# Last stage of a vision-transformer kernel: the layer norm's affine step and residual fused on VectorE over PSUM

## The reference, cut to what matters

```
z    = (h2 - mean(h2)) * rsqrt(var(h2) + eps)
r    = z + w_first * expert_out[first] + w_second * expert_out[second]
out  = h2 + (r - mean(r)) * rsqrt(var(r) + eps) * gamma + beta
```

## Time and profile before

| | us |
|---|---|
| median of 3 runs | 2032.84 |
| lowest, highest run | 2028.87, 2034.92 |
| span of the profiled execution | 2037.3 |
| first product of the last stage's matmuls used by DVE | 1877.96 |
| last DVE instruction of the stage ends | 2028.63 |

### The profile page before, as it was taken

The page is one execution under the profiler, slowest core; times in us unless marked ns, Lnnn a source line. Parts: engine busy times, 40 slices in busy tenths (PEclk is TensorE's granted clock), DMA queues, the critical chain, the costliest instruction groups (busy, mean ns, idle before and its releaser), DMA issues. The chain is left out here.

```text
span 2037.3 us, 49150 instructions
## 1 busy us (share of the span) xinstructions
PE 1498.2 (74%) x12152; PEld 991.7 (49%) x12153; DVE 1431.0 (70%) x3551; ACT 1376.4 (68%) x3956; POOL 1162.3 (57%) x1903
## 2 busy tenths in 40 slices
PE   6999957856656565663688885888865999994663
PEld 6999954411111111111344443555534988884553
DVE  2544559978777777776466666888876777774896
ACT  1323224429999999997799994777753766663885
POOL 2333330046666666662455552677775888884997
PEclk9999978955555555555555555555556999997786
DMA  7654310002222222221544445444433555554785
GB/s 293 258 231 193 160 39 1 1 32 83 85 75 76 76 87 75 84 78 49 136 138 150 143 146 152 132 154 154 154 123 107 140 140 137 146 144 143 224 271 159
DMA packets 184974, 263.32 MB, mean 129 GB/s; under 512 B 28372, under 2 KB 147363, under 8 KB 180328
## 3 DMA queue, kind: packets, MB, share of 16 engines
q1 hardware_dynamic: 137456, 202.16, 31.8%
q0 software_dynamic: 19840, 39.17, 5.4%
q10 hardware_dynamic: 27540, 20.52, 3.1%
HBM read 149.17 MB, written 108.01 MB: 126 GB/s over the span
## 5 line engine op out<-in xcount | busy, mean ns | idle before, releaser
L956 ACT ACTIVATE exps_summed<-s,neg_shift 128x197 f32<-128x197 f32 x1184 | 481.9, 535 | 32.4 <-POOL neg_shift L830 30.4
L956 ACT ACTIVATION_READ_ACCUMULATOR exps_summed<-s,neg_shift (+1 forms) x1184 | 339.0, 317 | 0.0
L993 DVE TENSOR_REDUCE score_max<-s 128x788 f32 (+3 forms) x320 | 285.9, 893 | 66.5 <-PE s L900 58.7
L1353 ACT ACTIVATE exps<-st,scalars 128x788 f32<-128x788 f32 (+1 forms) x320 | 246.4, 891 | 17.6 <-PE st L1262 17.5
L2034 POOL DMA_INDIRECT expert_sums<-y_tile,row_places x216 | 218.4, 1011 | 60.9 <-issue 28.9
L384 PE MATMUL mm<-w_tok,x_transposed 128*128 128x192 f32 x1176 | 209.4, 328 | 0.8 <-ACT x_transposed L345 0.8
L345 ACT COPY x_transposed<-tp 128x768 f32<-128x768 f32 x98 | 78.1, 798 | 176.8 <-PE tp L376 176.8
L384 PEld LDWEIGHTS mm<-w_tok,x_transposed 128*128 128x128 f32 x1176 | 190.8, 192 | 1.2 <-ACT x_transposed L345 1.2
L367 POOL TENSOR_SCALAR x_patches<-x_tile 128x768 f32<-128x768 f32 x98 | 81.4, 831 | 187.7 <-PE tp L376 172.1
L1173 POOL TENSOR_SCALAR probs<-exps 128x788 bf16<-128x788 f32 (+1 forms) x160 | 130.0, 819 | 102.3 <-ACT exps L1353 100.7
L900 PE MATMUL s<-k_int,qk_int 16*128 16x197 bf16 x768 | 98.7, 354 | 108.8 <-ACT exps_summed L956 106.0
(11 more groups left out here) (416 smaller groups left out, 4531.9 us busy)
## 6 DMA issues: line engine op xcount, KB each, us to landing
x_tile<-in_x SPq DMA_DIRECT2D x21, 1792.0 KB, 11.1
z_tile<-listed_rows SPq DMA_DIRECT2D x108, 196.0 KB
v_ints<-v_slots SPq DMA_DIRECT2D x32, 480.0 KB
v_slots_in<-v_ints SPq DMA_DIRECT2D x32, 480.0 KB, 3.6
q_ints<-qk_int SPq DMA_DIRECT2D x32, 295.5 KB
k_ints<-k_int SPq DMA_DIRECT2D x32, 295.5 KB
q_shifted<-q_ints SPq DMA_DIRECT2D x32, 295.5 KB, 3.6
k_ones<-k_ints SPq DMA_DIRECT2D x32, 295.5 KB, 4.3
```

The lines of the kernel that those rows point to most:

```text
L956: act.activation(gone[:, w % 2, k], ps[(turn + w) % 3][:, k, 0:SEQ], ACT.Exp, scale=alpha, bias=nb[:, s, to:to + 1], accum_out=p.lsum[:, b ...
L993: dve.tensor_reduce(columns(m, u), src, op=ALU.max, axis=AXL.X).then_inc(max_done, 1)
L1353: act.activation(ex[:, v % 4, 0:size(u)], src, ACT.Exp, scale=alpha, bias=p.col(C_LNSA)).then_inc(e_ready, 1)
```

## The change

`h2 + beta` is formed by POOL straight into `y_rows` before the statistics are there. The sum `weighted + z_in` goes back into its PSUM banks (four buffers now) and is read there by the statistics. DVE subtracts the mean and multiplies with gamma in one instruction per tile, in PSUM, and in the next body multiplies with the deviation's inverse and adds `y_rows` in one more instruction per tile. Both diagonals are built by ACT. The loads of `h_in` wait for `z_in` (`zd`) and POOL's sum (`based`) instead of the output, POOL's sum waits for the store of the block four before. The mean's negation, its product, ACT's normalisation, `res` and DVE's residual add are gone.

```diff
@@ finish: buffers @@
-    r = p.sb("res", [128, S, 4, D], F32, c)
-    nmean = p.sb("neg_mean3", [128, 2, 4], F32, c)
-    pw = [p.ps(f"weighted{k}", [128, 4, 256], F32, c) for k in range(2)]
+    pw = [p.ps(f"weighted{k}", [128, 4, 256], F32, c) for k in range(S)]
@@ sync @@
             if not is_block(n, range(S)):
-                need(sp, ys, n - 3)
+                need(sp, zd, n - 3)
+                need(sp, based, n - 3)
                 load_rows(sp, h_in[s], h2, s, src, n, nt)
@@ gpsimd @@
-        def affine(n, s, nt):
-            pool.wait_ge(ns, n + 1)
-            for k, (tt, rows) in enumerate(spans(nt)):
-                w = tt.stop - tt.start
-                rv = r[0:rows, s, tt]
-                pool.tensor_tensor(rv, rv, spread_tiles(gam[0:rows], w), ALU.mult).then_inc(zr, 1)
-                pool.wait_ge(zr, n + k + 1)
-                ins = pool.tensor_tensor(rv, rv, spread_tiles(bet[0:rows], w), ALU.add)
-            ins.then_inc(gb, 1)
-
         def body(n, s, i, nt):
-            pool.wait_ge(ves, n + 1)
-            need(pool, ns, n - 3)
-            pool.tensor_tensor(rs3[:, s, 0:nt], ve[:, 0:nt], half[:, 0:nt], ALU.pow).then_inc(rsd, 1)
-            pool.wait_ge(rsd, n + 1)
-            pool.tensor_tensor(nm3[:, s, 0:nt], nmean[:, s % 2, 0:nt], rs3[:, s, 0:nt], ALU.mult).then_inc(nms, 1)
-            if not is_block(n, [0]):
-                affine(n - 1, (s - 1) % S, 4)
+            need_apart(pool, h_in[s], landed(i, nt), tick_p)
+            need_apart(pool, o_out[s], 16 * i, tick_p)
+            for tt, rows in spans(nt):
+                ins = pool.tensor_tensor(y[0:rows, s, tt], h2[0:rows, s, tt], spread_tiles(bet[0:rows], tt.stop - tt.start), ALU.add)
+            ins.then_inc(based, 1)
+            need_apart(pool, ves, n + 1, tick_p)
+            need_apart(pool, ys, n - 1, tick_p)
+            pool.tensor_tensor(rs3[:, s % 2, 0:nt], ve[:, s % 2, 0:nt], half[:, 0:nt], ALU.pow).then_inc(rsd, 1)
@@ tensor @@
-            pe.wait_ge(first, n + 1)
-            pe.wait_ge(second, n + 1)
-            need(pe, rsum, n - 1)
+            pe.wait_ge(diag, n + 1)
+            need(pe, ys, n - 3)
@@ scalar @@
-            for t, rows in tiles(nt):
-                ins = act.activation(r[0:rows, s, t], r[0:rows, s, t], ACT.Identity, scale=rs3[0:rows, s, t:t + 1],
-                                     bias=nm3[0:rows, s, t:t + 1])
-            ins.then_inc(ns, 1)
@@
-                ins = act.activation(dgb[:, s % 2, t], p.idf[:], ACT.Copy, scale=p.wb[:, bass.ds(4 * n + t, 1)])
-            ins.then_inc(second, 1)
+                at = bass.ds(4 * n + t, 1)
+                act.activation(dga[:, s % 2, t], p.idf[:], ACT.Copy, scale=p.wa[:, at])
+                ins = act.activation(dgb[:, s % 2, t], p.idf[:], ACT.Copy, scale=p.wb[:, at])
+            ins.then_inc(diag, 1)
@@
-            if not is_block(n, [0]):
-                normal(n - 1, (s - 1) % S, 4)
-                if not is_block(n, [1, 2]):
-                    store(n - 3, (s - 3) % S, 4)
+            if not is_block(n, [0, 1]):
+                store(n - 2, (s - 2) % S, 4)
@@ vector @@
-                ins = dve.tensor_tensor(y[0:rows, s, tt], r[0:rows, s, tt], h2[0:rows, s, tt], ALU.add)
-                ins = dve.tensor_scalar(dga[:, s % 2, t], p.idf[:], p.wa[:, bass.ds(4 * n + t, 1)], None, ALU.mult)
-                ins = dve.tensor_tensor(r[0:rows, s, tt], pw[s % 2][0:rows, tt, 0:D], z[0:rows, s, tt], ALU.add)
+                ins = dve.tensor_tensor(pw[s][0:rows, tt, 0:D], pw[s][0:rows, tt, 0:D], z[0:rows, s, tt], ALU.add)
-                ins = dve.bn_stats(st6[0:rows, t], r[0:rows, s, t])
+                ins = dve.bn_stats(st6[0:rows, t], pw[s][0:rows, t, 0:D])
-            dve.tensor_scalar(nmean[:, s % 2, 0:nt], mv[:, 0:nt, 0], -1.0, None, ALU.mult)
-            dve.tensor_scalar(ve[:, 0:nt], mv[:, 0:nt, 1], LN_EPS, None, ALU.add).then_inc(ves, 1)
+            dve.tensor_scalar(ve[:, b, 0:nt], mv[:, b, 0:nt, 1], LN_EPS, None, ALU.add).then_inc(ves, 1)
+            for t, rows in tiles(nt):
+                ins = dve.scalar_tensor_tensor(out=pw[s][0:rows, t, 0:D], in0=pw[s][0:rows, t, 0:D], scalar=mv[0:rows, b, t, 0:1],
+                                               in1=gam[0:rows], op0=ALU.subtract, op1=ALU.mult)
+            ins.then_inc(scaled, 1)
+            if not is_block(n, [0]):
+                output(n - 1, (s - 1) % S, 4)
@@ vector, the new function @@
+        def output(n, s, nt):
+            b = s % 2
+            dve.wait_ge(rsd, n + 1)
+            dve.wait_ge(scaled, n + 1)
+            dve.wait_ge(based, n + 1)
+            for t, rows in tiles(nt):
+                ins = dve.scalar_tensor_tensor(out=y[0:rows, s, t], in0=pw[s][0:rows, t, 0:D], scalar=rs3[0:rows, b, t:t + 1],
+                                               in1=y[0:rows, s, t], op0=ALU.mult, op1=ALU.add)
+            ins.then_inc(ys, 1)
```

More of the change, by code:

```diff
@@ L2193, in finish @@
     z = p.sb("z_in", [128, S, 4, D], F32, c)
-    r = p.sb("res", [128, S, 4, D], F32, c)
     dga = p.sb("first_diagonals", [128, 2, 4, 128], F32, c)
     dgb = p.sb("second_diagonals", [128, 2, 4, 128], F32, c)
-    nmean = p.sb("neg_mean3", [128, 2, 4], F32, c)
-    pw = [p.ps(f"weighted{k}", [128, 4, 256], F32, c) for k in range(2)]
+    pw = [p.ps(f"weighted{k}", [128, 4, 256], F32, c) for k in range(S)]
     y = p.sb("y_rows", [128, S, 4, D], F32, c)
     st6 = p.sb("bn6c", [128, 4, 6], F32, c)
[L2201 to L2204, removed]
+    mv = p.sb("mv3", [128, 2, 4, 2], F32, c)
+    ve = p.sb("ve3", [128, 2, 4], F32, c)
     half = p.sb("half3", [128, 4], F32, c)
-    (init, w_in, zr, first, second, wsum, rsum, sts, ags, ves, rsd, nms, ns, gb, ys, zd, tick_v, tick_t) = p.sems(
-        p.ctx, "i", "init w_in zr first second wsum rsum sts ags ves rsd nms ns gb ys zd tick_v tick_t")
+    rs3 = p.sb("rstd3", [128, 2, 4], F32, c)
+    (init, w_in, diag, wsum, rsum, sts, ags, ves, rsd, scaled, based, ys, zd, tick_v, tick_t, tick_p) = p.sems(
+        p.ctx, "i", "init w_in diag wsum rsum sts ags ves rsd scaled based ys zd tick_v tick_t tick_p")
     h_in = p.sems(p.ctx, "i", "h_in0 h_in1 h_in2 h_in3")
@@ L2272, in body @@
             for t, rows in tiles(nt):
-                o = pw[s % 2][0:rows, t, 0:D]
+                o = pw[s][0:rows, t, 0:D]
                 nc.tensor.matmul(o, dga[0:rows, s % 2, t, 0:rows], ya[0:rows, s, t], start=True, stop=False)
@@ L2279, in scalar @@
     def scalar(act):
-        def normal(n, s, nt):
-            act.wait_ge(nms, n + 1)
-            for t, rows in tiles(nt):
-                ins = act.activation(r[0:rows, s, t], r[0:rows, s, t], ACT.Identity, scale=rs3[0:rows, s, t:t + 1],
-                                     bias=nm3[0:rows, s, t:t + 1])
-            ins.then_inc(ns, 1)
         def diagonals(n, s, nt):
@@ L2289, in diagonals @@
             for t, rows in tiles(nt):
-                ins = act.activation(dgb[:, s % 2, t], p.idf[:], ACT.Copy, scale=p.wb[:, bass.ds(4 * n + t, 1)])
-            ins.then_inc(second, 1)
-        act.wait_ge(p.weighed, 1)
-        diagonals(0, 0, 4)
+                at = bass.ds(4 * n + t, 1)
+                act.activation(dga[:, s % 2, t], p.idf[:], ACT.Copy, scale=p.wa[:, at])
+                ins = act.activation(dgb[:, s % 2, t], p.idf[:], ACT.Copy, scale=p.wb[:, at])
+            ins.then_inc(diag, 1)
         def store(n, s, nt):
@@ L2298, in store @@
             store_rows(act, o_out[s], dst, n, y, s, nt)
+        act.wait_ge(p.weighed, 1)
+        act.wait_ge(p.h2_out[0], 16 * (NBLK // 4) + 32)
+        for s in range(1, 4):
+            act.wait_ge(p.h2_out[s], 16 * (NBLK // 4))
+        diagonals(0, 0, 4)
         def body(n, s, i, nt):
@@ L2309, in body @@
             ins.then_inc(zd, 1)
-            if not is_block(n, [0]):
-                normal(n - 1, (s - 1) % S, 4)
-                if not is_block(n, [1, 2]):
-                    store(n - 3, (s - 3) % S, 4)
+            if not is_block(n, [0, 1]):
+                store(n - 2, (s - 2) % S, 4)
         blocks(act, body, S)
-        normal(NBLK, 0, 3)
-        store(NBLK - 2, 2, 4)
         store(NBLK - 1, 3, 4)
@@ L2326, in vector @@
         dve.wait_ge(ags, 1)
[L2328 to L2331, removed]
-                ins = dve.tensor_tensor(y[0:rows, s, tt], r[0:rows, s, tt], h2[0:rows, s, tt], ALU.add)
-            ins.then_inc(ys, 1)
-        def diagonals(n, s, nt):
-            need(dve, wsum, n - 1)
-            for t, rows in tiles(nt):
-                ins = dve.tensor_scalar(dga[:, s % 2, t], p.idf[:], p.wa[:, bass.ds(4 * n + t, 1)], None, ALU.mult)
-            ins.then_inc(first, 1)
-        diagonals(0, 0, 4)
+        def output(n, s, nt):
[6 more added lines that the diff above has]
+                                               in1=y[0:rows, s, t], op0=ALU.mult, op1=ALU.add)
+            ins.then_inc(ys, 1)
         def body(n, s, i, nt):
-            if not is_block(n, [NBLK]):
-                diagonals(n + 1, s + 1, 4)
```

(21 more changed lines are left out.)

1 line of the change is left out of this document (removed).

## The result

The changed kernel takes 2015.8 us (median of 4 runs, 2014.2 to 2016.8) against 2033.0 for the kernel before (2028.9 to 2034.9): a ratio of 0.992 [0.991, 0.994], faster by 0.8%, 17.2 us. I had forecast 2016.6. The profiled executions lie further apart than the medians, 2037.3 against 2013.5 us. The difference of 23.8 us splits up as follows; each part is the difference of two starts or ends in the two traces.

The account below looks back on a forecast made before the run. DVE's own queue was taken as the bound. Block 24's sum 7.9 us earlier and a tail of 5.5 instead of 14.3, less 0.4 for stores, gave 16.2 off 2032.84: 2016.6 us, range 2011 to 2027.

Parts of the forecast that it names:

- DVE's queue sets the period, 5.40 us: DVE, each block: eight fused instructions 2.62 us plus 2.79 for what stays, 5.40 in all, 0.49 less than now.
- PSUM costs next to nothing: DVE reading and writing PSUM: no extra cost taken; rival of 0.25 to 0.5 us a block, 2023 to 2029, chance 0.14.
- The two engines' collision goes: DVE and POOL hold each other up twice a block, some 1.3 us on DVE, 0.85 on POOL; this must stay away.
- the whole 1.37 of the negation: DVE, each block: the mean's negation, 1.37 us, counted within the 3.03 of 5.90 us that the change removes.
- The power: POOL, behind `ve` in each block: 0.86 us, against 1.71 beside DVE's residual add before the change.
- DMA is not the pace: Loads and stores: 291 GB/s needed, 329 seen; rival that DMA keeps a block at 5.89 us, 2024.4, chance 0.10.
- The loop's 7.9 and the tail's 8.8 us: Block 24's sum starts 7.9 us earlier; from it to DVE's last output 5.5 us instead of 14.3.
- The loads: PE's 28.4 us of waits for `sum_b`, put down to SP's queue order and hardly felt by DVE, would go.
- ACT covered, with 0.2 to 0.3 us to spare: ACT, each block: 4.2 us of work hidden behind DVE; rival that ACT sets 5.7 us a block, 2023.5, chance 0.11.
- What lies behind the last output stays: End of the span, after DVE's last output (2028.63 to 2037.3): unchanged by the change.
- 0.4 us for crowded stores: End of the stage: the last store follows 3 then 1 us behind the one before; 0.4 us charged.
- The first blocks start as before: Blocks 0 and 1 start about as now; until block 5 it takes 25.9 us, now 25.4.

Follow-up runs that it names:

- the third product's run: Changed kernel with `z_in` and DVE's sum left out; PE adds a third diagonal times `h_in` instead: 1995.1 us, ratio 0.981 to the kernel before.
- the loaded run: Changed kernel with four more copies per body on ACT, into a spare tile nothing reads: 2024.9 us, ratio 0.996 to the kernel before.

## Why the prediction was right, and where it was off

- **DVE's queue sets the period, 5.40 us.** It measured 5.38 in most blocks and 5.41 in the mean. The sum of the body was right in each term: fused instructions at 0.33 each, `ve` 0.08 of its own for 0.10, nothing stretched. Work put into this queue lengthened the period (5.41 to 6.54 with the diagonals), and work taken out shortened it (to 4.57 without the sum).
- **PSUM costs next to nothing.** The four statistics read it in 1.16 us (1.14 from SBUF), and the fused group that writes it took 1.40 beside 1.38 for the one that writes SBUF. The fixed cycles of "VectorE: DVE Perf Modes" in the Trainium skill (section on the TRN2 errata), 0.26 us a block by them, do not show; the rows decide.
- **The two engines' collision goes.** It does, and this is the mechanism. Taking one POOL operation from the kernel before gave 14.1 us of the median; the change's own parts show that two things are needed to profit on DVE: operands in PSUM (else 1.53 us a block come back) and the diagonals on ACT (else 1.13 do). The prediction books the whole 1.37 of the negation as work removed, though nearly 1.3 of it was waiting for POOL. DVE's own work per block grew, from some 4.6 us (5.90 less that wait; the kernel before without its affine step shows blocks of 4.63 and 4.67) to 5.38. The loop gained because the waiting went, not because DVE has less to do.
- **The power.** The prediction took 0.86 for it, from a power of three columns, and read 0.85 of delay out of 1.71. A block's power has four columns and takes 1.02, so the delay was 0.69. DVE did not feel the 0.16 more.
- **DMA is not the pace.** It moved 292 GB/s for the 291 forecast, and the third product's run shows that 345 are possible.
- **The loop's 7.9 and the tail's 8.8 us** came out at 8.1 and 8.7. About half of the gain is thus the end of the pipeline, a stretch of 14 us out of 2033.
- **The loads.** Their wait was rightly called not felt by DVE: with the old order the time is the same. That the order of SP's queue alone caused the wait is not borne out: with the old order in the changed kernel, 2.7 us of the 28.4 come back.
- **ACT covered, with 0.2 to 0.3 us to spare.** Covered it is; the term was too small. One body shows 0.39, and the loaded run says some 0.7.
- **"What lies behind the last output stays", and 0.4 us for crowded stores.** This was the missed step, off by 1.8 us: it gave 1.4 instead of costing 0.4. I had put that stretch down to the stores' landing without reading the queues' closing rows; it is POOL's DRAIN, counted from POOL's last instruction.
- **The first blocks start as before.** PE's first block came 1.1 us sooner in this execution, within the scatter of the other profiles. The second sum follows the first after 4.24 us, for 4.34 forecast.

The agreement of the median to 0.8 us is partly luck: in the traces the stage gained 18.3 us where the prediction has 16.2, and the runs of one kernel spread over 3 to 6 us.

## What to carry to other kernels

Where VectorE and GpSimd both work on SBUF alone, count what each holds up on the other before anything is mended, and remember that a stall moves on to the next such instruction of the queue; an operand kept in PSUM takes an instruction out of this, even with a scalar from SBUF. Read the drain at the end of a pipeline apart from its loop: operations that serialise there cost once what they hide in the loop, and here that was half the gain. Look at which queue ends last, and, if it is GpSimd's as here, let GpSimd finish early.

## What the runs showed of the hardware that I had not expected

- POOL's DRAIN ends 9.2 to 9.3 us after the last instruction of POOL's queue in all thirteen profiles, whatever that instruction is (an addition, a power, a write of 4 columns). With gamma and beta left out it is 10.8 us from the last arithmetic instruction (2001.31), but that queue closes with a semaphore increment that waits for ACT's last normalisation, which ends at 2002.76, and the DRAIN follows from 2002.9 for 9.22 us. No other queue's DRAIN outlasts POOL's here.
- Freeing an instruction of DVE that POOL holds up need not win its time: with the negation freed, the diagonals behind it were held 1.5 us instead.
- POOL's 1.8 us operations held DVE's instructions between SBUF tiles up, while its power beside them held none (fused instructions over SBUF, at most 0.42 us each) and was itself stretched, from 1.02 to 1.19 us there and to 1.7 us beside the residual add before the change.
- With a third product more on PE its granted clock was higher (1.00 from 1900 to 1970, that is the 2.4 GHz level throughout, against 0.85 in the loop after), and the extra products cost no more than 0.2 us of a block.
